# The causal mask copied by VectorE instead of multiplied in by TensorE, and queries rotated earlier

## The reference

```python
q, k, v = x @ wq, x @ wk, x @ wv            # 16 query heads, 4 key heads, 128 wide
k_ctx, v_ctx = ctx @ wk_ctx, ctx @ wv_ctx
q = rms_norm(q); k = rms_norm(k); k_ctx = rms_norm(k_ctx)
q = q * cos + rotate_half(q) * sin           # the same for k
scores = q @ concat(k_ctx, k).T / sqrt(128) + mask   # causal over the tokens' own keys
out = softmax(scores) @ concat(v_ctx, v) @ wo
x = x + tanh(g_xattn) * out
x = x + tanh(g_ffn) * down(silu(gate(ln(x))) * up(ln(x)))
```

## Time and profile before

| | |
|---|---|
| median of 3 runs | 312.08 us (311.5 to 312.15) |
| the profiled execution | 313.02 us, span 310.9 us |
| PE | 297.7 us busy, 96% |
| DVE | 231.8 us busy, 75% |
| ACT | 232.2 us busy, 75% |
| POOL | 181.6 us busy, 58% |
| granted TensorE clock, mean | 0.995 |

### The profile page before, as it was taken

The page is one execution under the profiler, slowest core; times in us unless marked ns, Lnnn a source line. Parts: engine busy times, 40 slices in busy tenths (PEclk is TensorE's granted clock), DMA queues, the critical chain, the costliest instruction groups (busy, mean ns, idle before and its releaser), DMA issues.

```text
span 310.9 us, 6576 instructions
## 1 busy us (share of the span) xinstructions
PE 297.7 (96%) x2239; PEld 236.7 (76%) x2239; DVE 231.8 (75%) x483; ACT 232.2 (75%) x893; POOL 181.6 (58%) x177
## 2 busy tenths in 40 slices
PE   7996999998999999999999999999999999988876
PEld 3453566765878888888888888888888888877765
DVE  1568999789899997779875787758775876676553
ACT  2377598986888778997977768896887768776632
POOL 1226596468648687366955586457755685556330
PEclk9999799999999999999999999999999999999999
DMA  7999000000000010000000010000000000000001
GB/s 200 391 388 393 13 17 2 0 1 2 18 2 1 1 36 2 0 2 8 30 0 2 0 37 0 2 1 20 0 3 2 0 19 2 2 0 19 0 0 36
DMA packets 6720, 12.84 MB, mean 41 GB/s; under 512 B 800, under 2 KB 4256, under 8 KB 6688
## 3 DMA queue, kind: packets, MB, share of 16 engines
q1 hardware_dynamic: 6688, 12.43, 11.4%
HBM read 11.38 MB, written 1.05 MB: 40 GB/s over the span
## 4 chain that ended last, share of the span: by engine, by line
PE 29%; ACT 28%; DVE 27%; issue 8%; POOL 5%; DMA 1%; SPq 0%; DVEq 0%; POOLq 0%
ACT probs L936 10%; ACT squares L772 7%; PE ps_y L446 4%; DVE row_max L1221 4%; DVE exp_bias L1224 4%; DVE q_sin L1086 4%; PE ps_kv L420 3%; ACT qt L856 3%; DVE q_rot L1082 3%; PE ps_attn L739 3%; ACT const L829 2%; PE ps_scores L695 2%; PE ps_transposed L432 2%; PE ps_probs L432 2%; ACT values L798 2%
## 5 line engine op out<-in xcount | busy, mean ns | idle before, releaser
L936 ACT ACTIVATE probs<-ps_scores,exp_bias,q_scale 128x128 f32<-128x128 f32 x128 | 56.9, 455 | 25.1 <-DVE exp_bias L1224 25.0
L1399 POOL TENSOR_TENSOR q_rot<-q_rot,q_sin 128x512 f32<-128x512 f32 x31 | 39.7, 1280 | 18.6 <-DVE q_sin L1086 18.4
L1443 POOL TENSOR_TENSOR probs<-probs,row_inv 128x512 f32<-128x512 f32 x32 | 36.2, 1131 | 18.5 <-DVE row_inv L1277 18.4
L1350 POOL TENSOR_TENSOR q_scale<-ssq_eps,minus_half 128x4 f32<-128x4 f32 x32 | 39.7, 1240 | 10.6 <-DVE ssq_eps L1247 9.8
L1361 POOL TENSOR_TENSOR fuse_lo<-fuse,fuse_hi 128x256 fp32r<-128x256 f32 x21 | 15.4, 732 | 41.3 <-ACT fuse_hi L781 41.3
L772 ACT ACTIVATE squares<-ps_q 128x128 bf16<-128x128 f32 x128 | 34.1, 292 | 7.0 <-PE ps_q L414 4.1
L739 PE MATMUL ps_attn<-pt,values 128*128 128x256 f32 x128 | 33.4, 383 | 0.0
L695 PE MATMUL ps_scores<-kt,qt 128*64 128x128 f32 x512 | 33.3, 273 | 0.0
L1082 DVE TENSOR_TENSOR q_rot<-ps_q,rope 128x512 f32<-128x512 f32 x31 | 21.3, 686 | 12.3 <-ACT squares L772 12.3
L695 PEld LDWEIGHTS ps_scores<-kt,qt 128*64 128x64 f32 x512 | 28.9, 137 | 0.0
L912 ACT ACTIVATE pt<-ps_probs 128x512 f32<-128x512 f32 x32 | 19.2, 600 | 12.5 <-PE ps_probs L432 12.5
(11 more groups left out here) (190 smaller groups left out, 843.1 us busy)
## 6 DMA issues: line engine op xcount, KB each, us to landing
q_raw<-in_wq_dram SPq DMA_DIRECT2D x4, 512.0 KB, 8.1
o_raw<-in_wo_dram SPq DMA_DIRECT2D x4, 512.0 KB, 11.6
ctx_t<-in_ctx_dram SPq DMA_DIRECT2D x8, 128.0 KB, 2.6
out_dram<-x_sb SPq DMA_DIRECT2D x8, 128.0 KB, 1.7
stage<-in_gate_w_dram SPq DMA_DIRECT2D x2, 384.0 KB, 9.9
stage<-in_up_w_dram SPq DMA_DIRECT2D x2, 384.0 KB, 10.9
x_sb<-in_x_dram SPq DMA_DIRECT2D x1, 768.0 KB, 13.0
stage<-in_down_w_dram SPq DMA_DIRECT2D x2, 384.0 KB, 13.2
```

What stands on the lines that cost most here:

```text
L936: last = nc.scalar.activation(probs[:, i, :], ps_s[:, i * P:(i + 1) * P], ACT.Exp, bias=exp_bias[:, i:i + 1], scale=q_scale[:, k % 2, i:i ...
L1350: return nc.gpsimd.tensor_tensor(dst, src, minus_half[:, 0:src.shape[1]], ALU.pow)
L1399: nc.gpsimd.tensor_tensor(q_rot[:, :, :], q_rot[:, :, :], q_sin[:, :, :], ALU.add)\
L1443: nc.gpsimd.tensor_tensor(probs[:, :, :], probs[:, :, :], row_inv[:, :].unsqueeze(2).broadcast_to([P, 4, P]), ALU.mult).then_inc(probs_rea ...
```

## The change

Four things are done.

1. From step 12 on, the mask matmuls are left out. VectorE copies a table mask_all (128 x 128, repeated over the four heads) into the scores' bank, behind ot_lo and, at j = 2, behind xn, and TensorE's score matmuls wait for mask_set and add to what they find. mask_all is cleared by GpSimd and filled by VectorE before step 0.
2. In steps 12, 15, 16, 19, 20, 23, 24, 27, 28 and 31 (ROTATE_FIRST) VectorE rotates the queries of the next step right behind the mask, ahead of xn at j = 3 and of gating and fusing. It waits for the projection (q_made) and no longer for ScalarE's squares; the squares wait for q_sin instead. GpSimd's addition goes ahead of fuse_lo in these steps.
3. In all steps, xt_lo (j = 0) and k_var (j = 2) go behind row_max and exp_bias.
4. In all steps TensorE waits for the squares before it projects into ps_q again, and ssq_eps waits for them too.

```diff
+ROTATE_FIRST = tuple(k for k in range(12, STEPS) if k % GROUPS in (3, 0))
+MASK_ON_VECTOR_FROM = 12
+        mask_all = sb("mask_all", [P, P])
...
 # TensorE
                         pe.wait_ge(q_sin_ready, step(u, k) + 1)
+                        pe.wait_ge(q_squared, step(u, k) + 1)
...
-                    for r in range(2):
+                    if step(u, k) >= MASK_ON_VECTOR_FROM:
+                        pe.wait_ge(mask_set, step(u, k) - MASK_ON_VECTOR_FROM + 1)
+                    for r in range(2 if step(u, k) < MASK_ON_VECTOR_FROM else 0):
...
 # ScalarE, square_queries
-                    act.wait_ge(q_made, step(u, k + 1) + 1)
+                    if step(u, k) in ROTATE_FIRST:
+                        act.wait_ge(q_sin_ready, step(u, k + 1) + 1)
+                    else:
+                        act.wait_ge(q_made, step(u, k + 1) + 1)
...
 # VectorE
+            def fill_mask():
+                dve.wait_ge(mask_cleared, 1)
+                for r in range(2):
+                    rows = slice(r * LEN, (r + 1) * LEN)
+                    last = nc.vector.tensor_copy(mask_all[rows, rows], const[rows, C_MASK:C_MASK + LEN])
+                last.then_inc(mask_filled, 1)
+            def set_mask(s):
+                if s == MASK_ON_VECTOR_FROM:
+                    dve.wait_ge(mask_filled, 1)
+                dve.wait_ge(exp_ready, s)
+                nc.vector.tensor_copy(four(ps_s), mask_all[:, :].unsqueeze(1).broadcast_to([P, HPG, P])).then_inc(mask_set, 1)
...
 # VectorE, rotate_queries
-                    dve.wait_ge(q_squared, step(u, k + 1) + 1)
+                    if step(u, k) in ROTATE_FIRST:
+                        dve.wait_ge(q_made, step(u, k + 1) + 1)
+                    else:
+                        dve.wait_ge(q_squared, step(u, k + 1) + 1)
...
 # VectorE, one_step, behind ot_lo and xn of j = 2
+                if is_step(u, k) and step(u, k) >= MASK_ON_VECTOR_FROM:
+                    set_mask(step(u, k))
+                if at_step(u, k) in ROTATE_FIRST:
+                    rotate_queries(u, k)
...
-                rotate_queries(u, k)
+                if at_step(u, k) not in ROTATE_FIRST:
+                    rotate_queries(u, k)
...
 # VectorE, one_step: xt_lo (j == 0) and k_var (j == 2) move from ahead of row_max to behind exp_bias
...
 # VectorE, ahead of ssq_eps
+                    dve.wait_ge(q_squared, step(u, k + 1) + 1)
...
 # GpSimd: add_rotated holds the addition (L1399)
+                if at_step(u, k) in ROTATE_FIRST:
+                    add_rotated(u, k)
                 fuse_rest(u, FF_LATE.get(k - 1))
...
+                if at_step(u, k) not in ROTATE_FIRST:
+                    add_rotated(u, k)
```

More of the change, by code:

```diff
@@ L211, in build @@
         half_set = sem("half_set")
+        mask_cleared, mask_filled, mask_set = sem("mask_cleared"), sem("mask_filled"), sem("mask_set")
         tables_ready = sem("tables_ready")
@@ L1200, in one_step @@
                                             ALU.subtract).then_inc(x2_lo_ready, 1)
+                if at_step(u, k) in SHORT_OF_VECTOR:
+                    attention_low(u, k)
+                if is_step(u, k):
+                    dve.wait_ge(scores_made, step(u, k) + 1)
+                    nc.vector.tensor_reduce(row_max[:, :], four(ps_s), AX.X, ALU.max).then_inc(max_ready, 1)
+                    dve.wait_ge(max_ready, step(u, k) + 1)
+                    dve.wait_ge(q_scale_ready, step(u, k) + 1)
+                    nc.vector.scalar_tensor_tensor(exp_bias[:, :], row_max[:, :], -1.0, q_scale[:, k % 2, :],
+                                                   ALU.mult, ALU.mult).then_inc(bias_ready, 1)
                 if j == 0 and is_tile(u, m + 1) and tile(u, m + 1) >= TOKENS_SPLIT_FROM:
@@ L1213, in one_step @@
                         .then_inc(ks_var_ready, 1)
[L1215 to L1225, removed]
                 if j == 2 and is_tile(u, m + 2):
@@ L1343, in _ @@
             scales()
+            fill_mask()
             run_steps(dve, one_step)
@@ L1366, in fuse_rest, with add_rotated @@
                         .then_inc(result_ready, 1)
+            def add_rotated(u, k):
+                if is_step(u, k + 1):
+                    pool.wait_ge(q_sin_ready, step(u, k + 1) + 1)
+                    nc.gpsimd.tensor_tensor(q_rot[:, :, :], q_rot[:, :, :], q_sin[:, :, :], ALU.add)\
+                        .then_inc(q_rot_ready, 1)
             def quantize_store(i):
@@ L1464, in _ @@
             nc.gpsimd.memset(minus_half[:, :], -0.5).then_inc(half_set, 1)
+            nc.gpsimd.memset(mask_all[:, :], 0.0).then_inc(mask_cleared, 1)
             first_roots()
```

## The result

The changed kernel takes 312.23 us, median of 20 runs; the kernel before, in 20 runs beside it, 311.51. The ratio is 1.0025, 95% interval 1.0013 to 1.0036: slower by 0.25%, some 0.8 us. I had forecast 0.66 faster. The profiled execution takes 313.5 us, its span is 311.3.

The account below looks back on a forecast made before the run. TensorE's own order bounds it up to step 27, then a loop through ScalarE, VectorE and GpSimd in the last tile. Terms 0.24 + 0.20 - 0.21 - 0.92 - 0.16 + 0.19 = -0.66 gave 311.4 us; range 309.6 to 312.9.

Parts of the forecast that it names:

- Mask matmuls, 0.08 a step: Steps 12 to 31: dropping the mask matmuls saves TensorE 0.08 us a step, 1.6 over 20 steps, bounds 0 and 0.14.
- The copy's 0.60, k_sin late by as much, 4 x 0.47 = 1.88: Steps 14, 18, 22, 26: VectorE's copy delays k_sin 0.60, so the value projection waits 0.47 more each, +1.88 us.
- The lead: Third steps of a tile: what leads up to xn was to run some 0.13 us earlier relative to TensorE.
- The other steps with the late rest of step 16 and the six small waits, -1.68: Other 12 steps of 12 to 27: mask -0.96, step 16's late output rest -0.36, six waits of 0.06 -0.36.
- The scores need the mask only some 0.8 us after it is there, so the new wait on mask_set costs nothing: TensorE's score matmuls: the copied mask was to be ready some 0.8 us early, so their wait costs nothing.
- the last tile at -1.10: Steps 28 to 31: -0.21 in 28, -0.92 in 29, mask -0.16 in 30 and 31, +0.19 for step 31's copy.
- Step 28, -0.21, and 29, -0.92: Last tile: early rotation brings exponentials 1.05 earlier; queries' turn stops waiting (-0.13, -0.08), step 29's 0.84 wait goes (-0.92 with mask).
- k_var behind exp_bias, +0.24 in step 2: Step 2: k_var after a blocked exp_bias starts k_inv at 41.93 instead of 41.69; +0.24, between 0 and 0.4.
- The lost race of xn: Rival, chance 0.10: GpSimd's addition beats xn in last steps; steps 15, 19, 23 wait 0.65 each, +2.0, 312.8 us.
- Nothing comes of it: Rival, chance 0.14: last tile's gain of 1.1 fails, by blocked exp_bias or mask copies making steps 29 and 30 late; 312.1.

Follow-up runs that it names:

- r1: Changed kernel, but in steps 14, 18, 22 and 26 TensorE multiplies the mask in again as before; 310.86 us, ratio 0.9964.
- r10: Changed kernel without the early rotation (ROTATE_FIRST empty), mask copies kept from step 12 on; 314.52 us, ratio 1.0100.
- r2: Changed kernel with the mask copy ahead of the outputs' rest (ot_lo) in steps 28 to 31; 311.27 us, ratio 0.9986.
- r3: Changed kernel with no mask copies, every mask on TensorE; early rotation, moved instructions and added waits stay; 310.10 us, ratio 0.9950.
- r7: Changed kernel with copies only in steps 15-17, 19-21, 23-25 and 27, and xt_lo of steps 4 and 8 back ahead of row_max; 309.25 us, ratio 0.9914.
- r9: r7 with both added waits for the squares (TensorE's and VectorE's) only where the rotation is ahead; 308.40 us, ratio 0.9901.
- r11: r7 with only TensorE's added wait limited to steps behind an early rotation, VectorE's kept everywhere; one run, 309.13 us.
- r8: Changed kernel with the copy of steps 14, 18, 22 and 26 behind the rotation of the keys; one run, 312.86 us.

## Why the prediction was wrong

Its sum was -0.66; by the trace it is +0.38 (span 0.40, of which 0.02 lie ahead of step 0), and by the medians +0.72. Term by term, in its order:

- *Mask matmuls, 0.08 a step:* right; -0.07 to -0.09 in steps 15, 19, 23 and 27. Of the Trainium skill's rule in TensorEngine Tiling (Array Packing), Key Properties, no run here shows more: the rest of the 0.13 may be the drain or the weight load in the open.
- *The copy's 0.60, k_sin late by as much, 4 x 0.47 = 1.88:* right, 1.77, and r1 shows that it is the copy. The copy measured 0.68, with the next instruction 0.59 behind its start. The split was 0.60, 0.39, 0.39 and 0.39. The lead came in another place than I had said: in steps 18, 22 and 26 attention's copies and xn start no earlier behind the turn, but xn is 0.18 shorter, as GpSimd's multiplication beside it is further on (r10); step 14 has no such lead.
- *The other steps with the late rest of step 16 and the six small waits, -1.68:* -1.75 and +0.28, that is -1.47. I had hidden the copy in step 12 behind the wait that the early rotation removes, without counting that gating then stands 1.8 us of VectorE's work behind the rest instead of none; feed-forward waited 0.20 for the fused piece.
- *"The scores need the mask only some 0.8 us after it is there, so the new wait on mask_set costs nothing":* **this step failed.** It is true where I had looked, in steps 12 to 27, and I carried it to the last tile, where TensorE reaches the scores without an output projection. There TensorE stood idle for 0.27, 0.50 and 1.75 until the mask came, about 1.0 of the last beyond its wait for qt. I had put the last tile at -1.10 (-0.21 - 0.92 - 0.16 + 0.19); it gave -0.30, which is 0.80 of the 1.04 between -0.66 and +0.38. r2 moves the four copies ahead of ot_lo and changes nothing else: the last tile gives -1.29, and the time is 0.96 lower. For step 31 I had asked what the copy delays behind it on VectorE (+0.19), and not what waits for it.
- *Step 28, -0.21, and 29, -0.92:* the mechanism of the early rotation was right: in r3, without the copies, they give 0.13 and 1.05. With the copies they give +0.09 and -0.53, and with the copies ahead of ot_lo (r2) -0.24 and -1.00, near the forecast. Step 30 gave 0.57 unforeseen, the wait for xn that a later step 29 hides: time moved from one step to the next.
- *k_var behind exp_bias, +0.24 in step 2:* k_inv did start late (42.02, 41.69, with 0.12 of it the general lead), but only 0.08 reached step 3. The real price was in step 9, 0.23. Of it 0.08 is the moves', as xt_lo ahead of ssq_eps pushed the latter behind the start of GpSimd's store (1.54 instead of 0.16; r7 takes this away), and 0.15 is the added wait's on TensorE (r9, r11). I had given the added waits no price.
- *The lost race of xn:* it was won, as counted: in step 23 xn starts at 225.01, GpSimd's addition at 225.18, and xn takes 0.41.

No rival was the one that came. "Nothing comes of it" named mask copies that make steps 29 and 30 as late as before, at 312.1, but as a risk to the gain and not as this wait; that 312.1 lies near 312.23 is luck, as steps 29 and 30 together were 1.10 shorter. Two of the rivals' figures don't follow from their terms: the lost race adds 2.0 to 311.4, which is 313.4 and not 312.8, and a last tile whose gain of 1.1 fails is 312.5 and not 312.1.

## What to carry to other kernels

When work moves to another engine, its result becomes a wait in every place where it is used, also at the ends of the schedule, where the work that hid it may be missing: read the slack there separately. Put the moved instruction where its own inputs are ready, not behind one that waits for a third engine, and move it only in those steps in which the new engine isn't what the old one waits for; ten copies of twenty were worth 0.9 us, and the other ten cost 2.8 (312.23 less 309.39). Give added semaphore waits only to the steps that need them.

## What was not expected of the hardware

In these runs the copy into PSUM is not held up by GpSimd, whichever of the two starts first. In r2 (263.33) it starts ahead of GpSimd's multiplication and takes 0.67; in step 27 of r8 it starts behind it, lies inside it and takes 0.68. ssq_eps, a much smaller operation within SBUF, took 1.54 where it started behind a GpSimd store (changed kernel, step 8). First r8, then the changed kernel:

```profile
256.82 1.04 POOL L1495 TENSOR_TENSOR probs<-probs,row_inv 128x512 f32<-128x512 f32 x1
256.97 0.68 DVE L1077 COPY ps_scores<-mask_all 128x512 f32<-128x512 f32 x1
...
96.24 1.84 POOL L1419 TENSOR_TENSOR w_down<-stage,quant_m 128x768 fp32r<-128x768 f32 x1
96.57 1.54 DVE L1287 TENSOR_SCALAR ssq_eps<-ssq 128x4 f32<-128x4 f32 x1
```

The Trainium skill, SBUF — State Buffer, Who interferes with whom, has this: an operation of VectorE with one input in SBUF and outside the two-port modes does not contend with GpSimd, and a tensor_scalar within SBUF can. The traces agree with both.

A wait for a semaphore that had already been reached was not free in two places: 0.15 us ahead of the projection of step 9 on TensorE, and 0.28 us of "issue" on VectorE in step 13, which made step 14 longer by 0.26. In the other steps from 4 on the same waits cost nothing that can be seen (0.02 or less).
